# Three reciprocal roots of a recurrent block as powers on GpSimd, with a new order of work

## What is computed

```
xn = (x - mean) / sqrt(var + 1e-5)                  # per token: "token variance"
r, w, k, v, g, a, ma, mk2 = projections of mixes of xn and the token before
kk = k + tanh(xk @ kkk_w1) @ kkk_w2
kk = kk / max(norm(kk over the 64 channels of a head), 1e-12)   # "key norm"
for each token t:                                   # per head, state S is 64 x 64
    S = S * exp(w_t) + (S a_t) b_t^T + v_t k_t^T ;  y_t = S r_t     # a = -kk, b = kk * a
y = (y - mean) * rsqrt(var + 0.00064) per head      # "head variance"
y = (y * ln_w + ln_b + sum(r*k*faaaa) * v) * g @ w_output
out = x + y * silu(ffn(xn)),  ffn(z) = (silu(z @ wg) * (z @ wu)) @ wd
```

## Time and profile before

| | |
|---|---|
| median of 3 runs | 1801.68 us (1797.99 to 1804.48) |
| the profiled execution | 1809.13 us, span 1807.7 us |
| PE busy | 1625.3 us, 90% |
| DVE, ACT, POOL busy | 1234.1, 1207.0, 480.0 us (68%, 67%, 27%) |
| mean granted TensorE clock | 0.941 |

### The profile page before, as it was taken

How to read it: one execution, slowest core, us unless ns; L and a number is a source line. 1 busy time by engine, 2 the same in 40 slices (tenths; PEclk the granted TensorE clock), 3 DMA queues, 4 the chain that set the end, 5 groups by cost and what they waited for, 6 DMA issues and landing times.

```text
span 1807.7 us, 47903 instructions
## 1 busy us (share of the span) xinstructions
PE 1625.3 (90%) x20224; PEld 1116.4 (62%) x20224; DVE 1234.1 (68%) x2608; ACT 1207.0 (67%) x2047; POOL 480.0 (27%) x388
## 2 busy tenths in 40 slices
PE   1679999999998999999899999999999999999966
PEld 0255757667575766757576675757667575765745
DVE  3476777677676777767677676777777676776713
ACT  1838758584875858587584958768585875849512
POOL 0414132241313224141332414132241413324000
PEclk9879999999998999999899999999999999999968
DMA  3011020211202021110201112030211203011110
GB/s 132 12 17 31 9 51 14 50 22 30 42 8 51 14 46 25 30 42 6 54 15 40 31 30 42 3 58 14 45 26 30 42 3 58 14 40 19 35 25 25
DMA packets 251430, 57.83 MB, mean 32 GB/s; under 512 B 223696, under 2 KB 250704, under 8 KB 251088
## 3 DMA queue, kind: packets, MB, share of 16 engines
q1 hardware_dynamic: 241936, 41.95, 12.3%
q10 hardware_dynamic: 9280, 12.81, 2.0%
HBM read 36.38 MB, written 18.35 MB: 30 GB/s over the span
## 4 chain that ended last, share of the span: by engine, by line
PE 77%; SPq 6%; DVE 5%; ACT 4%; DMA 4%; issue 3%; POOL 0%; DVEq 0%; ACTq 0%
PE bank L356 16%; PE bank L506 16%; PE bank L516 10%; PE bank L481 7%; DMA Y<-in_x 3%; PE chunk L612 3%; PE chunk L584 3%; PE chunk L559 3%; PE bank L455 3%; PE chunk L568 2%; PE bank L468 2%; PE bank L634 2%; PE bank L461 2%; PE chunk L598 2%; SPq L1342 1%
## 5 line engine op out<-in xcount | busy, mean ns | idle before, releaser
L506 PE MATMUL bank<-xT,wu 128*128 128x256 f32 x768 | 219.8, 423 | 0.0
L506 PE MATMUL bank<-xT,wg 128*128 128x256 f32 x768 | 202.1, 400 | 18.3 <-DVE KS L962 18.3
L1305 POOL TENSOR_TENSOR SF<-ST,CT 128x256 f32<-128x256 f32 x128 | 97.4, 761 | 450.4 <-DVE ST L1168 450.4
L839 ACT ACTIVATE sg<-bank 128x512 f32<-128x512 f32 x96 | 57.1, 595 | 228.9 <-PE bank L506 228.5
L516 PE MATMUL bank<-wd,hT 128*128 128x256 f32 x768 | 186.5, 393 | 0.0
L1246 POOL TENSOR_TENSOR big<-KS,xT 128x512 f32<-128x512 f32 x64 | 75.2, 1197 | 407.1 <-DVE KS L962 407.1
L506 PEld LDWEIGHTS bank<-xT,wg 128*128 128x128 f32 x768 | 142.8, 196 | 60.1 <-DVE KS L962 30.7
L356 PE MATMUL bank<-big,W 128*128 128x512 f32 (+1 forms) x320 | 167.2, 657 | 13.1 <-POOL big L1246 6.5
L506 PEld LDWEIGHTS bank<-xT,wu 128*128 128x128 f32 x768 | 151.3, 209 | 36.6 <-issue 11.4
L516 PEld LDWEIGHTS bank<-wd,hT 128*128 128x128 f32 x768 | 143.2, 193 | 22.0
L356 PE MATMUL bank<-KS,W 128*128 128x512 f32 x320 | 144.2, 597 | 0.0
(11 more groups left out here) (161 smaller groups left out, 3559.9 us busy)
## 6 DMA issues: line engine op xcount, KB each, us to landing
smalls<-in_x SPq DMA_DIRECT2D x32, 256.0 KB, 3.0
Y<-in_x SPq DMA_DIRECT2D x32, 256.0 KB, 3.7
out<-fsil ACTq DMA_DIRECT2D x32, 256.0 KB, 2.2
scrA<-AM SPq DMA_DIRECT2D x64, 64.0 KB, 1.9
hat<-scrB SPq DMA_DIRECT2D x32, 128.0 KB, 3.3
hat<-scrF SPq DMA_DIRECT2D x32, 128.0 KB, 3.1
KE<-scrA SPq DMA_DIRECT2D x64, 32.0 KB, 2.3
scrT<-KE SPq DMA_DIRECT2D x16, 128.0 KB, 1.7
```

The lines of the kernel that those rows point to most:

```text
L506: q = pe.matmul(o[:, TT_ * n2:TT_ * n2 + TT_], w[:, h, 128 * (n + n2):128 * (n + n2) + 128], x_now[:, h], start=(h == 0), stop=(h == NH - 1))
L839: act.activation(sg[:, :], ring.tile(key)[:, :], ACT.Silu).then_inc(*sg_ready.up)
L1305: pool.tensor_tensor(SF[:, :, :, :], ST[:, :, :, :], fade[:, c].unsqueeze(3).to_broadcast([128, B, NH, N]), ALU.mult).then_inc(*faded.up)
```

## The change

The functions Sqrt, Ln and Exp of the three roots on ACT and the two reciprocals on DVE go. In their place POOL adds the epsilon (`tensor_scalar`, for the two variances) and raises to the power -0.5 (`tensor_tensor` with ALU.pow, whose second operand is one column that holds -0.5, broadcast). The maximum of the key norm on DVE and the product kk on POOL stay. The division of the head variance by 64 moves into the scale of the square. All four ORDER strings are new.

```diff
-         "pool": ("FFFFFFFFDBFEXEBKBXBBBBBL")}
+         "pool": ("BOFFFFFFFFXDFEEBKKBXBLBBBLB")}
...
@@ act_program
             def norm(t):
-                act.wait_ge(*mv_ready(t))
-                act.activation(rstd[:, :], mv[:, :, 1], ACT.Sqrt, bias=eps[:, 0:1]).then_inc(*x_std.up)
-                yield "std"
...
-                act.wait_ge(*rn_max(t))
-                act.activation(rn[:, :, :], rn[:, :, :], ACT.Ln).then_inc(*rn_ln.up)
-                yield "rn_ln"
-                act.wait_ge(*rn_ln(t))
-                act.activation(rn[:, :, :], rn[:, :, :], ACT.Exp, scale=-0.5).then_inc(*rn_ready.up)
-                yield "rn"
...
-                act.activation(sq, Y[:, :, :], ACT.Square).then_inc(*y_sq.up)
+                act.activation(sq, Y[:, :, :], ACT.Square, scale=N ** -0.5).then_inc(*y_sq.up)
...
-                act.wait_ge(*y_var(t))
-                act.activation(st2[:, :], st2[:, :], ACT.Sqrt, bias=eps[:, 1:2], scale=1.0 / N).then_inc(*y_std.up)
-                yield "groupnorm"
@@ dve_program
-                dve.wait_ge(*x_std(t))
-                dve.reciprocal(rstd[:, :], rstd[:, :]).then_inc(*rstd_inv.up)
...
-                dve.wait_ge(*y_std(t))
-                dve.reciprocal(st2[:, :], st2[:, :]).then_inc(*y_inv.up)
@@ pool_program
             def norm(t):
+                pool.wait_ge(*mv_ready(t))
+                pool.tensor_scalar(rstd[:, :], mv[:, :, 1], LN_EPS, None, ALU.add).then_inc(*x_std.up)
+                pool.wait_ge(*x_std(t))
+                pool.tensor_tensor(rstd[:, :], rstd[:, :], minus_half[:, 0:1].to_broadcast([128, NM]), ALU.pow).then_inc(*rstd_inv.up)
+                yield "root"
...
             def key(t):
+                pool.wait_ge(*rn_max(t))
+                pool.tensor_tensor(rn[:, :, :].rearrange("p h n -> p (h n)"), rn[:, :, :].rearrange("p h n -> p (h n)"),
+                                   minus_half[:, 0:1].to_broadcast([128, NH * COLS]), ALU.pow).then_inc(*rn_ready.up)
+                yield "root"
                 pool.wait_ge(*rn_ready(t))
                 pool.tensor_tensor(kk[:, :, :], kk[:, :, :], rn[:, :, :], ALU.mult).then_inc(*kk_ready.up)
...
             def output(t):
-                yield from ()
+                pool.wait_ge(*y_var(t))
+                pool.tensor_scalar(st2[:, :], st2[:, :], GN_EPS, None, ALU.add).then_inc(*y_std.up)
+                pool.wait_ge(*y_std(t))
+                pool.tensor_tensor(st2[:, :], st2[:, :], minus_half[:, 0:1].to_broadcast([128, NM * H]), ALU.pow).then_inc(*y_inv.up)
+                yield "root"
```

More of the change, by code:

```diff
@@ L51 @@
 CTOT = _at
[L53 to L57, removed]
-         "pool": ("FFFFFFFFDBFEXEBKBXBBBBBL")}
+ORDER = {"pe": ("NOFNONNNNNNOFNNFKFORKRRKVBVBKNNKVBBVBBBVBBVBBBNBBNNBBNEBNBBBNBBNBBNBBNBNNBNBBXXBBXNBNLBBXXBBXXBXBBNX"
+            "BBXXNLX"),
+         "act": ("NNNFKFFFFFFRDDKRRKVBVBKKKEOBBVVBOBBVVDVBVBXXXBNNBBBXBBNBBXBBNLBXLBBXLBXBBXBBXNLX"),
+         "dve": ("OBOFOBNBBBBNBOBFFFFFFFBBBBBBBBBODDDDDKKNDDKDDKBBEBBXLEEXXBEEBXBXBXNXXBXXXBLNXXXBXXXXBXXNXBXXXXBXXXXX"
+             "XBXLLXXBB"),
+         "pool": ("BOFFFFFFFFXDFEEBKKBXBLBBBLB")}
 NB = 4
@@ L127, in program @@
         mask = sb("mask", [128, 64], U32)
-        eps = sb("eps", [128, 4])
+        one = sb("one", [128, 2])
+        minus_half = one[:, 1:2]
         wg = sb("wg", [128, NH, DH])
@@ L216, in program @@
         vu_ready, sqk_ready = signal("vu_ready", NH), signal("sqk_ready", 3)
-        lora_ready, mixa_ready, hk_ready, gh_ready, rn_ln, rn_ready, kk_ready = (
-            signal(n) for n in ("lora", "mixa_ready", "hk_ready", "gh_ready", "rn_ln", "rn_ready", "kk_ready"))
+        lora_ready, mixa_ready, hk_ready, gh_ready, rn_ready, kk_ready = (
+            signal(n) for n in ("lora", "mixa_ready", "hk_ready", "gh_ready", "rn_ready", "kk_ready"))
         mkz_ready, em_ready, kem_ready, k_fin, b_fin, rk_ready = (signal(n) for n in ("mkz", "em_ready", "kem", "k_fin", "b_fin", "rk_ready"))
@@ L248, in program @@
                                                        hat[1][:, :, :, :].rearrange("p q x t -> p (q x t)"))]
-        NSET = 13
+        NSET = 11
         x_in, x_out = d["x"], d["out"]
@@ L822, in decays @@
                 act.wait_ge(*dz_exp(t))
-                act.activation(az[:, :, :], az[:, :, :], ACT.Ln, bias=eps[:, 2:3]).then_inc(*dz_ln.up)
+                act.activation(az[:, :, :], az[:, :, :], ACT.Ln, bias=one[:, 0:1]).then_inc(*dz_ln.up)
                 yield "ln"
@@ L1212, in dve_program @@
             n_set = 0
-            for level, col in ((LN_EPS, 0), (GN_EPS, 1), (1.0, 2), (0.0, 3)):
-                dve.memset(eps[:, col:col + 1], level).then_inc(s_set, 1)
+            for level, col in ((1.0, 0), (-0.5, 1)):
+                dve.memset(one[:, col:col + 1], level).then_inc(s_set, 1)
                 n_set += 1
```

## The result

The changed kernel takes 4328.32 us (median of 4 runs, 4327.3 to 4330.59), the kernel before 1803.08 us (4 runs): a ratio of 2.4012, 95% interval 2.3951 to 2.4074. The forecast was 1763 us with 1725 to 1890 as its range.

The account below looks back on a forecast made before the run. PE, busy 90% of the span, was taken as the bound. Gains of 34.5 us from gaps, 2.6 in the first tile and 1 in the last tile's tail made 38, giving a median of 1763 us, range 1725 to 1890.

Parts of the forecast that it names:

- The dear power: Rival: POOL's power between the fades of steps 1 and 2 slows PE from 5.4 us on; 1870 or 2060 us; chance 0.33.
- P: Length of POOL's key norm power on 128x1024, taken as 5 us; free up to 5.4 us.
- Chain: From the head sums through power, kk, DVE's statistics, b and rk: 12.1 us + P.
- Stretch that covers it: PE's work between the head sums and the head sums of rk in the new order: 17.5 us.
- the first tile: Key norm chain at the start, where PE waits: kk at 83.7 instead of 86.3 us, 2.6 us gained.
- The small power: POOL's two instructions on 16 numbers for the head variance's root: 0.9 us; at 3 us, transposes late about 1 us per tile.
- The order's gain: Shorter PE gaps at band, mixes and recurrence: 2.3 us per tile, 34.5 us for 15 tiles.
- the hole behind the band: PE's gap between band and corner at the inverse, filled by a value projection: 0.79 us gained per tile.
- The mixes: PE's gaps at the output projection and first mix: 1.0 of 2.6 us gained per tile, 1.6 left.
- The clock comes back: Rival: mixes and inverse run at clock 1.00, 45 us more gained, 1718 us; chance 0.07.
- The lock: Ports shared by POOL and DVE: DVE's dm waits for the end of a long power; 0.6 us in the sum.
- the rule on operations: About three operations per cycle on POOL: 5 us would be 18 operations, 12 us 42; taken as a sign for a dear power.

Follow-up runs that it names:

- key_product: Changed kernel with the key norm's power (128x1024 on POOL) replaced by a product of the same shape: 1777.4 us, ratio 0.9856 to the kernel before.
- all_product: Changed kernel with the key norm's power and both variances' small powers replaced by products: 1763.67 us, ratio 0.9783 to the kernel before.
- key_pow32: Changed kernel with the key norm's power over only the first 32 of 1024 columns: 1781.05 us, ratio 0.9868 to the kernel before.
- old_order_key_pow: Kernel before, its order kept, with only the key norm as a power of 128x1024 on POOL: 4373.11 us, ratio 2.4220.
- key_pow256: Changed kernel with the key norm's power over only the first 256 of 1024 columns: 2367.38 us, ratio 1.3134 to the kernel before.
- key_pow64: Changed kernel with the key norm's power over only the first 64 of 1024 columns: 1875.87 us, from one execution.
- new_order_old_functions: Changed kernel's new order, with all three roots by ACT's functions and DVE's reciprocals as before: 1951.0 us, ratio 1.0804 to the kernel before.
- key_act_late: Changed kernel with the key norm's logarithm and exponential back on ACT, the logarithm directly ahead of the exponential: 1832.29 us, ratio 1.0161 to the kernel before.

## Why the prediction was wrong

**The step that failed is the price of the power.** "Between them I take 5 us, by the row of the product, which is the nearest; both ends stay in the range." What the runs show in its place is 163.3 us, 33 times the value taken and 7 times the end called the upper one. That end was a count of passes at the product's speed, and nothing in the rows said that a power is made of ten passes, or that each costs what a product does; by time it is 70 products. A bound that rests on a guessed count isn't a bound. Nor did the range hold even that one: by the prediction's own sum 24 us give 2060 us, and the range ended at 1890, a power of 13. The dear power's place and its threshold were right, and 0.33 stood on it, but at P = 12 and 24.

**Everything around P held.** Start of the power: 6.5 us after the head sums, 6.45 measured in most sections. Chain: 12.1 + P, measured to 0.2 us where the power starts then. Stretch that covers it: 17.5 us, 17.6 here. Free up to 5.4 us: the wait is P less 5.7 with 64, 256 and 1024 columns. With P = 163.2 the prediction's own sum gives 1801.7 - 38 + 157.8 * 15 + 158.2 (the first tile) = 4289 us, in which the power makes 2525. The 39 us to 4328 close by the table: between key_product and the changed kernel the wait of L469 rose from 7.8 to 2520.5, 12.5 less than the sum had; PE's busy time rose by 34.6 between the two; the change without its key power gains 26.1 in spans where the sum had 38, so 11.9 more; and the profiled execution of before was 7.5 over its median. Together 41.5, 2 too many.

**The small power.** 0.9 us taken, 2.92 and 0.26 for the addition measured. "Were the small power as dear as 3 us, the transposes would be late instead, by about 1 us per tile" came true in the new order: 1.4 us per tile. It was the smaller sign of the same mistake.

**The order's gain: right in total by luck, wrong in kind.** all_product, which has a product of 1.9 us in place of the power and no dear small one, is the nearest to the kernel of the forecast, and takes 1763.67 us against 1763. But 34.5 us were to come from gaps and none from the clock. Its idle time is 22.5 us less than before and its busy time 19.7 less, for the same products: the second half came from the clock, which in the steady window is 0.98 where it was 0.96:

```profile
200.00:1650.00 1450.00, 1382.24 (x17671) 950.41 (x17670) 1029.74 (x2228) 921.15 (x1646) 478.15 (x403) 0.98 0.15 31
```

Place by place: the hole behind the band is gone (12.6 us before, 0.8 now), as forecast. The mixes wait 25.3 us (L507 and L387) where they waited 32.9: the 1.6 us per tile that were to remain did, but the 1.0 gained was read from a section where the residual was late, and over 15 tiles it is 0.5. In the recurrence L584 and L559 lost 14.5 us (17.6 to 3.1), and L613 brought back 16.3. "For the clock I take nothing: both places keep a gap" was the too careful term, and made up for a gain in gaps that was half too large. In windows of 4 us from 200 to 1650 us the kernel before falls under a clock of 1.00 at the inverse in all 14 tiles and at the mixes in 10; all_product in 7 and 2, key_product in 4 and none. So both places kept a gap and most of their low clock went all the same: the rival *The clock comes back*, which had 0.07, came true in part.

**The first tile.** It was to gain 2.6 us at P = 5, with the power from 76.3 us on. The first power starts at 81.2 us, since POOL waits for DVE's maximum (the 1.3 us <-DVE KS L988 in its group). In key_pow32, whose first power takes 6.3 us, kk ends at 89.9 instead of 86.3, but the head sums of rk start at 92.58 us, as before (92.64), because rk had waited for something else there: b was done at 87.5, and rk started at 91.18. So a power of that length costs the first tile nothing and gains nothing, where 2.6 us were to come; with a product in its place (key_product) they start at 89.88.

**The lock.** The prediction had dm wait for the end of a long power. It took 80.7 us and ended 83.4 us into a power of 163.24, at 51%. By the Trainium skill ("SBUF — State Buffer", section "SBUF: two separate sides") the shared pair of ports is locked for the whole instruction. Beside a power the trace doesn't agree: half of the long one held DVE, and of the power of 256 columns nothing did. Beside products it agrees here as in the earlier trace rows: in key_product dm begins beside the second of two products (1.89 and 2.35 us), takes 2.73 us instead of 1.22, and ends 1.1 us behind it. In the changed kernel the hold cost nothing of its own, since b waited for kk anyway; in old_order_key_pow it stood on PE's path.

**The estimate from the rule on operations.** By the Trainium skill ("GPSIMD Engine Reference", section "Performance versus the Vector engine"), three operations per cycle, 163.2 us for 1024 columns would be, as an estimate at that page's 1.2 GHz, some 570 operations for each. No run here shows how many it is, so the rule is neither confirmed nor refuted; it could not have given a price without that count.

## What to carry to other kernels

An instruction that no trace shows has no upper bound until it has been timed; the way to one is a run of it at a few small sizes (here 4 and 16 columns would have told the 1024), before an order is built around it. Work out the slack of its place separately, as 17.5 less 12.1 here: that number held whatever the price (5.4 worked out, 5.7 measured), and says at once which size could be afforded (about 31 to 33 columns, by the line of the sizes). And compare the engine's whole work with the tile: 163.2 us of power alone are more than the 104.7 us of a tile before. The squared norms are 1024 columns of 128 partitions only because each stands 64 times; the 2048 different ones would fill 16 columns of all 128 partitions, which by the line of the sizes are 2.95 us (an estimate, without what it takes to bring them there and back). A form that is compact in partitions but keeps its 1024 columns would save nothing, since the price is per column. None of this was tried.

## What the runs showed of the hardware

- GpSimd's power: 0.41 us and 0.159 us per column, linear from 4 to 1024 columns, the same on 64 and 128 partitions. In a product of 1024 columns it is 0.0023 us per column.
- A DVE operation with two inputs in SBUF was held until 83.4 us into a power of 1024 columns (163.2 us), in both orders, and not at all by one of 256 or 64 in the steady part. Why half is open; the number of partitions isn't the reason (64 and 128 alike), nor is the point at which it begins (0.2 to 5.5 us into the long power, 2.7 to 5.6 us into that of 256 columns).
- These waits of PE cost their length and then a stretch at a lower clock, which isn't longer for a longer wait. The 8 us behind a wait of 157.5 us in the changed kernel, and behind one of 35.4 us in key_pow256, with what follows (behind one of 4.8 us in key_pow64, 869.3 to 877.3 us, the clock is 0.69):

```profile
2077.00:2085.00 8.00, 7.84 (x84) 0.72 0.01 2
2085.00:2120.00 35.00, 34.62 (x696) 1.00 0.08 13
```

```profile
1537.70:1545.70 8.00, 7.84 (x108) 0.81 0.01 2
1545.70:1580.00 34.30, 34.02 (x674) 1.00 0.08 12
```

- So 8 us at 0.72 lose 2.2 us, an estimate from the first row; 16 of them are 36, and PE's busy time in the changed kernel is 34.6 us over key_product's. Many short waits cost more in this way than one long one: new_order_old_functions has 74.7 us more idle time than key_product and 97.1 more busy time, and one of its tiles (907 to 1023 us) has three stretches under 1.00 in windows of 4 us, down to 0.59, 0.55 and 0.73. The 34.0 us more busy time of key_act_late are too near to the 26 us between key_product's own executions to be read, and of the 47.9 us of key_pow256 these stretches give 24 (16 times the 1.5 us of 8 us at 0.81, an estimate); the rest is open.
- In the new order the clock rose without less idle time: key_product idles 0.9 us more than the kernel before and is busy 27.0 less, and all its executions have a clock of 0.964 to 0.978, all those of before 0.933 to 0.948. The low stretches went at the inverse and at the mixes, as the windows above say. Which of the gaps' changes did it wasn't tested one by one.
